# Cross-attention and quantised feed-forward on one core: tokens laid out with features on partitions, LayerNorm 1 folded into Wq and the query bias, token parts made a step ahead

## The reference, cut to what matters

```python
def _layernorm(x, eps=1e-05): ...           # (x - mean) / sqrt(var + eps) over the 512 features
def _ln(t, w, b): ...                       # the same over the 32 features of a head, with gain and shift

def xattn(x, y):
    y_main, y_dca = y[:, :-16], y[:, -16:]
    q = _ln((x @ Wq + bq) by head, qn_w, qn_b)
    k = _ln((y_main @ Wk + bk) by head, kn_w, kn_b);   v = y_main @ Wv + bv
    k_dca = _ln(keys of (y_dca @ Wkv_dca + bkv_dca), kn_dca_w, kn_dca_b);   v_dca = its values
    ctx = softmax(q k' * SCALE) v + softmax(q k_dca' * SCALE) v_dca      # two separate softmaxes
    return ctx @ Wo + bo

x = x + xattn(_layernorm(x), ctx_1024)
x = x + fake_quant(relu(fake_quant(_layernorm(x)) @ fake_quant(kernel) + fake_quant(bias)))   # 8 bits
```

## Time and profile before

| | |
|---|---|
| median of 3 runs | 368.29 us (367.71 to 371.18) |
| the profiled execution | 370.66 us, of which the span from the first to the last instruction is 368.8 us |
| busy share of the span | TensorE 87%, weight loads 70%, VectorE 85%, ScalarE 60%, GpSimd 47% |
| DMA | 39.14 MB moved, mean 106 GB/s; HBM read 17.15 MB |
| from the k_t transposes of batch 2 (78.08 us) to those of batch 14 (302.51 us) | 224.43 us for 12 steps, 18.70 us each |

### The profile page before, as it was taken

The page is one execution under the profiler, slowest core; times in us unless marked ns, Lnnn a source line. Parts: engine busy times, 40 slices in busy tenths (PEclk is TensorE's granted clock), DMA queues, the critical chain, the costliest instruction groups (busy, mean ns, idle before and its releaser), DMA issues.

```text
span 368.8 us, 7583 instructions
## 1 busy us (share of the span) xinstructions
PE 319.3 (87%) x2338; PEld 257.3 (70%) x2353; DVE 315.0 (85%) x804; ACT 222.5 (60%) x444; POOL 174.3 (47%) x261
## 2 busy tenths in 40 slices
PE   1498989799989999999898999999998999868732
PEld 0345657688877878787787888878787878566620
DVE  2987899799979899989898998989998999975664
ACT  3357886366666767676758585848584856552501
POOL 5201513327281828282828281828282837281620
PEclk9999899699999999999999999999999999998985
DMA  8870458507070909190909082828292616180002
GB/s 267 263 265 1 82 121 142 125 29 163 15 177 11 194 22 191 34 199 18 195 17 189 31 139 81 128 93 130 92 135 84 123 54 123 54 145 2 28 0 85
DMA packets 36451, 39.14 MB, mean 106 GB/s; under 512 B 8760, under 2 KB 27452, under 8 KB 36412
## 3 DMA queue, kind: packets, MB, share of 16 engines
q1 hardware_dynamic: 36044, 38.40, 48.2%
q10 hardware_dynamic: 368, 0.27, 0.3%
HBM read 17.15 MB, written 4.72 MB: 59 GB/s over the span
## 4 chain that ended last, share of the span: by engine, by line
PE 52%; DMA 9%; SPq 7%; issue 7%; DVE 3%; ACT 2%; POOL 0%; ACTq 0%; DVEq 0%
PE bank L1323 26%; SPq L372 7%; PE bank L1440 7%; DMA q_stack<-q_lo 7%; PE bank L1409 4%; PE bank L1596 4%; PE bank L1606 2%; PE bank L1420 2%; PE bank L1421 2%; PE bank L1463 2%; PE bank L1493 1%; DMA k_stack<-k_lo 1%; ACT k_hi L606 1%; PE bank L1498 1%; PE bank L1455 1%
## 5 line engine op out<-in xcount | busy, mean ns | idle before, releaser
L1440 PE MATMUL bank<-v_aug,prob_store 128*128 128x66 f32 x512 | 68.6, 278 | 3.4 <-ACT prob_store L744 3.4
L511 POOL TENSOR_TENSOR k_lo<-wkv_raw,k_hi 128x448 f16<-128x448 f32 x16 | 16.7, 1042 | 113.8 <-issue 105.9
L1440 PEld LDWEIGHTS bank<-v_aug,prob_store 128*128 128x128 f32 x512 | 64.4, 195 | 5.9 <-ACT prob_store L744 4.6
L1056 DVE TENSOR_REDUCE neg_max<-bank 128x4 f32<-128x448 f32 (+1 forms) x128 | 45.2, 416 | 9.9 <-PE bank L1409 9.9
L755 ACT ACTIVATE wkv_raw<-bank,affine 128x448 f32<-128x448 f32 (+1 forms) x32 | 22.4, 747 | 42.4 <-PE bank L1493 42.1
L744 ACT ACTIVATE prob_store<-bank,exp_scale 128x512 f32<-128x512 f32 x64 | 41.6, 677 | 4.9 <-PE bank L1421 4.8
L530 POOL TENSOR_TENSOR finals<-seg_out 128x128 f32<-128x128 f32 x64 | 34.4, 546 | 13.7 <-DVE seg_out L1069 13.4
L1420 PE MATMUL bank<-q_stack,k_stack 128*128 128x128 f16 x256 | 33.9, 220 | 1.9 <-ACT maxT L606 1.9
L1421 PE MATMUL bank<-maxT,sel 128*128 128x128 bf16 x256 | 33.7, 219 | 0.0
L1420 PEld LDWEIGHTS bank<-q_stack,k_stack 128*128 128x128 f16 x256 | 26.4, 104 | 6.1 <-issue 3.9
L1069 DVE TENSOR_TENSOR seg_out<-bank,rden 128x256 f32<-128x256 f32 x64 | 27.2, 424 | 3.8 <-POOL finals L530 1.7
(11 more groups left out here) (213 smaller groups left out, 876.9 us busy)
## 6 DMA issues: line engine op xcount, KB each, us to landing
x_in<-in_x SPq DMA_DIRECT2D x16, 256.0 KB, 4.9
q_stack<-q_hi SPq DMA_DIRECT2D x32, 128.0 KB, 3.7
q_stack<-q_lo SPq DMA_DIRECT2D x32, 128.0 KB, 4.6
k_stack<-k_hi SPq DMA_DIRECT2D x32, 128.0 KB, 3.3
k_stack<-k_lo SPq DMA_DIRECT2D x32, 128.0 KB, 4.3
out<-finals SPq DMA_DIRECT2D x16, 256.0 KB, 3.8
y_in<-in_ctx SPq DMA_DIRECT2D x16, 128.0 KB, 4.6
y_dcaT<-in_x SPq DMA_DIRECT2D x8, 256.0 KB, 4.3
```

Of the source, the lines that this page charges most:

```text
L1056: v.tensor_reduce(neg_max[:, HG * gr:HG * (gr + 1), seg], s4[:, :, lo:hi], AX.X, ALU.max, negate=True).then_inc(max_ready.sem, 1)
L1440: last = mm(bank[6 + gr % 2][:, VW * h:VW * (h + 1)], probs[:, gr % 2, h], v_aug[:, Bt.parity, HG * gr + h], start=True, stop=True)
```

## The change

Six things change together.

1. The host passes four more arrays (`laid_out`): tokens and main context rows with features on partitions (`tokens_T`, 128 x 736 a batch), the DCA rows the same way (`dca_T`), the six norm vectors in one row, and the bias and norm columns as 14 columns. The transposes of tokens and DCA rows on TensorE, and `setup_columns`, go.
2. `xT_hi`, `yT_hi` are copies by ScalarE of what was loaded (`high_context`, `high_stream`); they are double-buffered and made for batch L, a step ahead of their use. `xT_lo`, `yT_lo` move from VectorE to GpSimd (`low_context`, `low_stream`), for batch A.
3. x goes into the q product raw. LayerNorm 1's mean is taken out of Wq once: `setup_sums` (TensorE) makes the mean over the 512 input features of every column of the head-centred Wq, `level_queries` (VectorE) subtracts it. Its scale is applied when the query bias is added (`biased_queries`). `x_norm` is not made any more; the statistics are still taken from `x_in`, so x is now loaded twice for this stage.
4. The DCA part of Wkv_dca is loaded in two halves and its keys are centred partly on GpSimd (`centred_dca`).
5. SyncE issues the token loads of a step after the residual and DCA value loads, not before the store of the step.
6. `x_plus` and `f_intT` get other buffers.

```diff
 # SyncE, per step
-                if L is not None and L.has(2):
-                    prev = L.back(2)
-                    sp.wait_ge(*xn_ready.of(prev))
-                    sp.dma_start(x_in[:, L.parity], x[L.index()]).then_inc(x_loaded.sem(L), 16)
-                    sp.wait_ge(*yT_ready.of(prev))
-                    sp.dma_start(y_in[:, L.parity], ctx[L.index()]).then_inc(y_loaded.sem(L), 16)
+                def tokens():
+                    if L is not None and L.has(2):
+                        prev = L.back(2)
+                        sp.wait_ge(*ln1_steps.of(prev, 2))
+                        sp.dma_start(x_in[:, L.parity], x[L.index()]).then_inc(x_loaded.sem(L), 16)
+                        for read in (xhi_ready, xlo_ready, yhi_ready, ylo_ready):
+                            sp.wait_ge(*read.of(prev))
+                        sp.dma_start(xy_in[:, L.parity], xyT[L.index()]).then_inc(xy_loaded.sem(L), 16)
+
+                if N is None or not N.has(2):
+                    tokens()
...
                     if N.has(2):
                         residual()
                         dca_values()
+                        tokens()
...
 # GpSimd
+                def low_tokens(lo, hi, src, loaded, hi_ready, used, done):
+                    pool.wait_ge(*loaded)
+                    pool.wait_ge(*hi_ready.of(A))
+                    if A.has(1):
+                        pool.wait_ge(*used.of(A.back(1)))
+                    g.tensor_tensor(lo[:].rearrange("p c n -> p (c n)"), src,
+                                    hi[:, A.parity].bitcast(FP32).rearrange("p c n -> p (c n)"), ALU.subtract
+                                    ).then_inc(done.sem, 1)
...
                         pool.wait_ge(*kstack_in.of(N.back(1)))
                         dca_columns(k_hi, kdca_hi)
                         dca_columns(k_lo, kdca_lo)
-                        low(k_lo, k_n, k_hi, kn_ready, khi_ready, kstack_in, klo_ready, MAIN)
+                if A is not None and not A.first():
+                    low_context()
+                    low_stream()
+                if N is not None and not N.first():
+                    low(k_lo, k_n, k_hi, kn_ready, khi_ready, kstack_in, klo_ready, MAIN)
...
 # ScalarE
+                def high_context(b):
+                    act.wait_ge(*((first_context.sem, 16) if b.first() else xy_loaded.of(b)))
+                    if b.has(2):
+                        act.wait_ge(*v_ready.of(b.back(2)))
+                    copy(flat(yT_hi[:, b.parity]), context_in(b.parity)).then_inc(yhi_ready.sem, 1)
...
+                if L is not None and L.has(2):
+                    high_context(L)
+                    high_stream(L)
                 if N is not None:
                     if N.first():
                         setup_dca(0)
...
+                if L is not None and L.second():
+                    high_context(L)
+                    high_stream(L)
...
 # VectorE
+            def level_queries():
+                dve.wait_ge(wqsum_ready.sem, 1)
+                level = bank[0][:, :].unsqueeze(1).to_broadcast([P, XC // 2, D])
+                for half in range(2):
+                    part = slice(XC // 2 * half, XC // 2 * (half + 1))
+                    v.tensor_tensor(wq_raw[:, part], wq_raw[:, part], level, ALU.subtract).then_inc(wq_levelled.sem, 1)
...
-                    v.tensor_tensor(q_raw[:, A.parity], bank[2][:, :], bias_full[:, 0], ALU.add
-                                    ).then_inc(qraw_ready.sem, 1)
+                    if A.first():
+                        dve.wait_ge(bias_copied.sem, 2)
+                    dve.wait_ge(*ln1_rstd.of(A))
+                    v.scalar_tensor_tensor(q_raw[:, A.parity], bank[2][:, :], x_rstd[:, A.parity:A.parity + 1],
+                                           bias_full[:, 0], ALU.mult, ALU.add).then_inc(qraw_ready.sem, 1)
...
 # TensorE
+            def setup_sums():
+                pe.wait_ge(tiles_made.sem, 8)
+                for c in range(XC):
+                    pe.wait_ge(wq_centred.sem, 1 if c < XC // 2 else 2)
+                    last = mm(bank[0][:, :], per_token[:].to_broadcast([P, P]), wq_raw[:, c, :], start=c == 0, stop=c == XC - 1)
+                last.then_inc(wqsum_ready.sem, 1)
...
-                    for c in range(YC):
-                        last = tr(bank[1][:, P * c:P * (c + 1)], y_in[:, p, P * c:P * (c + 1)], ident[:])
-                    last.then_inc(yT_ready.sem, 1)
...
-                    for c in range(XC):
-                        last = tr(bank[0][:, P * c:P * (c + 1)], x_norm[:, p, P * c:P * (c + 1)], ident[:])
-                    last.then_inc(xT_ready.sem, 1)
```

More of the change, by code:

```diff
@@ L339, in _ @@
                      bias_parts[:, part])
+            sp.dma_start(x_in[:, 1], x[1]).then_inc(x_loaded.sems[1], 16)
+            sp.dma_start(xy_in[:, 1], xyT[1]).then_inc(xy_loaded.sems[1], 16)
             load(fk_in, fk_raw[:], chunked(ffn_kernel))
+            load(wdv_in, wd_raw[:, :, 1], chunked(Wkv_dca)[:, :, D:2 * D])
             load(wo_in, wo_raw[:], chunked(Wo))
@@ L618, in _ @@
             load(biases_in, bias_heads[2 * H:3 * H], bkv_dca[0:D].rearrange("(h d) -> h d", d=HD))
-            for j in range(2):
-                load(dca_in, y_dca[:, j], ctx[8 * j:8 * (j + 1), MAIN:, :])
             s.preload_act_table_set("natural_log_exp_and_others")
@@ L811, in step @@
                     setup_dca(1)
-                if L is not None and not L.second():
-                    token_statistics()
+                if L is not None and L.has(2):
+                    token_statistics(L)
                 if Bt is not None:
@@ L1165, in step @@
                     setup_ffn_bias()
-                if A is not None:
-                    low_part(yT_lo, yT_hi, bank[1][:, 0:CD], yhi_ready, v_ready, A, ylo_ready)
-                    if A.first():
-                        setup_queries()
-                if Bt is not None and Bt.first():
-                    low_part(xT_lo, xT_hi, bank[0][:, :], xhi_ready, q_ready, A, xlo_ready)
+                if A is not None and A.first():
+                    setup_queries()
                 if Bt is not None:
@@ L1629 @@
     arrays, args = {}, []
-    for name in _INS:
-        a = np.ascontiguousarray(inputs[name])
+    for name, a in [(name, inputs[name]) for name in _INS] + list(laid_out(inputs).items()):
+        a = np.ascontiguousarray(a)
         arrays[f"in_{name}"] = a
```

270 lines of the change are left out of this document (129 added, 141 removed).

## The result

The changed kernel takes 379.74 us (median of 4 executions, 378.3 to 381.5) against 368.63 us: a ratio of 1.0269, 95% interval 1.0215 to 1.0323. It is slower by 2.7%; the forecast was no change (367.6 us), and the time lies outside the range of 360.0 to 373.5. The profiled execution took 380.59 us, with a span of 378.7. Every ratio in this document leaves out the executions that took over 1.5% more than the fastest of the same kernel, so for e5, e10 and e12, where that matters, the median of all executions stands beside it.

The account below looks back on a forecast made before the run. Steps were taken as bound by a loop from k_t transposes over the stacks' DMAs and `scores(0)` to the next k_t. Setup +7.7 us, steps -8.4 us: 368.29 - 0.7 = 367.6 us, range 360.0 to 373.5.

Parts of the forecast that it names:

- I take 0.15 us a step, near the low end, because the products have that cover.: Steps: low parts on GpSimd delay VectorE's k and q head products, about 1 us of cover; 0.15 us lost a step.
- rival C: Steps: GpSimd and VectorE collide every time, losing 0.85 us a step and cancelling the gain; 376.0 us, chance 0.12.
- The loads behind the stacks: Steps: x_in moves from behind q_lo to behind the DCA values; about 0.3 us a step of shorter wait.
- can't turn into a longer wait at `scores(0)`: Steps: token transposes, 0.65 us of TensorE, stand behind that wait, so removing them shortens the loop without lengthening it.
- Setup up to batch 0's squares: Setup, start to batch 0's squares: cost +1.1 us, bounds -0.6 and +2.8.
- These nearly cancel: Setup: earlier weights, loads and bias against added matmuls and VectorE passes; batch 0's q product within half a microsecond of before.
- The ScalarE term: Setup: two copies of batch 1 (1.0 us) stand ahead of the square of q on ScalarE; cost +1.1 us.
- Batch 1's k product: Setup: waits for GpSimd's low parts behind both DCA key parts; starts at about 45.8, 6.4 us later.
- Rival B: Faster: setup hides one of its two stalls, costing 3.5 us, and steps give 0.85 each; 361.6 us, chance 0.32.
- ScalarE's wait for batch 3: Setup, step 0: some 4 us wait for xy_in at about 60 us; batch 2's k_t transposes come 7.7 us later.
- Rival D: Steps: token loads land too late for ScalarE every time, or freed time doesn't come; 373.6 us, chance 0.08.
- The tail: End of the kernel: no token work is left in it, so nothing changes.

Follow-up runs that it names:

- e5: Changed kernel with the edits of e2, e3 and e4 together: ratio 0.9705 to the kernel before, median of all executions 360.71 us against 370.0.
- e10: e5 with batch 0's `low_stream()` and `token_scale(A)` behind `centred_dca()` on GpSimd: ratio 0.9695 to the kernel before, median of all executions 366.63 us.
- e12: e5 again, unchanged, on another chip: ratio 0.9712 to the kernel before, median of all executions 360.09 us against 370.11.
- e4: Changed kernel; from batch 2 yT_lo back on VectorE, xT_lo on GpSimd only after VectorE's q_t product: 372.2 us, ratio 1.0048 to the kernel before.
- e9: e5 with a step's token loads issued at its start, behind q_lo of the step before: 362.41 us, ratio 0.9788 to the kernel before.
- e7: Changed kernel with a step's token loads issued at its start, behind q_lo of the step before: 381.18 us, ratio 1.0317 to the kernel before.
- e15: Changed kernel, unchanged, run for a second profile: 48.9 us from the last k_t transposes to the end.
- e2: Changed kernel with batch 1's low parts ahead of k_lo of batch 0 on GpSimd: 372.57 us, ratio 1.0088 to the kernel before.
- e3: Changed kernel; in step 0 ScalarE copies batch 3's high parts behind the copy of maxT: 376.71 us, ratio 1.0188 to the kernel before.
- e11: Changed kernel with both low parts subtracted twice on GpSimd from batch 2 on: 384.97 us, ratio 1.0417 to the kernel before.

## Why the prediction was wrong

**The loss is the setup's, and the steps don't pay for it.** The prediction was 7.7 us of setup against 8.4 us of steps. Measured in three profiles each: 11.5 against 2.9. The steps' gain missed by 5.5 us and the setup by 3.8.

**The term that failed: "I take 0.15 us a step, near the low end, because the products have that cover."** The cover is there: with the collision gone the step is 17.78 us (e4), a gain of 0.91 where 0.85 was booked. But I priced what the two 512-column products would lose. They lose nothing (1.08 us each, as before). What GpSimd's low parts hold are the 32-column operations ahead of them, and the forecast priced none of these: 1.4 us a step, 1.6 with the one that the FFN scaling holds, of which 0.67 are left after the cover. That is 8.0 us in 12 steps, 6.2 more than booked, and the larger part of the error. It was in my own rows: the earlier trace rows is exactly a small operation, stretched from 0.19 to 1.02 us by a GpSimd operation of 1.04. I had it down as a sign for rival C and still gave C 0.12. The Trainium skill (page "SBUF — State Buffer", section "SBUF: two separate sides") states that a VectorE operation with two SBUF inputs and a GpSimd operation that reads SBUF exclude one another for the whole instruction. Applied to the small operations, that rule was the better forecast. The traces agree with it: L1079 and L1081 end 0.05 us behind the GpSimd operation that they meet, and the maxima, which read PSUM, take 1.41 us for four beside xT_lo in e4.

**Rival C** named the mechanism and nearly its size (0.85 us lost a step, 0.67 measured), and its 376.0 us is the nearest of the four. It was short by the setup (3.8 us); the steps gained a little where it gave them nothing.

**The loads behind the stacks** were booked at about 0.3 us of the 0.85. They are worth 0.18 where the loop is the bound (e9), and next to nothing in the changed kernel (e7). That the transposes' removal "can't turn into a longer wait at `scores(0)`" held: the idle there went from 0.87 us to nothing. It turned into a wait further on, at the q_t transposes.

**Setup up to batch 0's squares:** +1.1 booked, +2.8 measured at k_t of batch 0. "These nearly cancel" was wrong: the q product of batch 0 started at 28.00, 29.45 and 28.95 us in the three profiles of the changed kernel, against 26.54, 25.28 and 28.67, 2.0 us later by the means. The ScalarE term was nearly right: from the q product to its square it is 0.9 us more by the means, 1.1 booked. What holds the q product differs between the profiles. In the first one the new mean over the input features (`setup_sums`, L1404) takes 3.67 us, and the levelling (L1002) starts only at 24.38, behind VectorE's list of small operations, of which GpSimd had stretched L974 to 1.72 us from 0.16 before; the centring of Wq ahead of it had taken 3.35 us (2.89 before, 2.36 in e10). e10 shows that one of these two can be taken away, and that the other place then pays. In the other two profiles the same sums take 6.41 and 6.58 us, and the levelling waits for them. TensorE's and VectorE's timelines of e15:

```profile
18.85 6.41 PE L1404 MATMUL bank<-wq_raw,per_token 128*128 128x512 f32 x8 [1.42 <-DVE wq_raw L936]
...
25.29 2.35 DVE L1002 TENSOR_TENSOR wq_raw<-wq_raw,bank 128x1024 f32<-128x1024 f32 x2 [0.60 <-PE bank L1404]
```

That is what the prediction had as its upper bound of 2.8, the sums at twice their time. Why they take it in some executions no row shows: the granted clock reads 1.00 from 16 to 30 us in all three. The first four DCA products of the kernel before vary in the same way, 3.50, 1.98 and 3.78 us.

**Batch 1's k product:** right. Predicted at 45.8 with GpSimd's yT_lo as the releaser; it started at 47.40 (the 1.6 are the first stretch's error), and e2 shows that nothing else was behind those 6.3 us. Rival B, which needed this wait or the next to be hidden, falls.

**ScalarE's wait for batch 3:** right in place and size (about 4 us at about 60; 4.40 us up to 66.93). But it was priced as if all of it reached the steps; e3 took it out and got 2.2 us at batch 2's k_t transposes. In that profile a longer stretch at half clock follows; that it took the place of the wait is likely, not shown.

**Rival D,** ScalarE waiting for xy_in in every step: the wait is there (12.3 us in all) and costs nothing (e7).

**The tail** was right at no change; the first profile of the changed kernel alone would have charged it with 2.8 us.

**What was open** is the share of the clock in the setup. Apart from the stall ahead of batch 1's k product (e2), the three stretches before batch 2 have half-clock windows in some executions and not in others, of both kernels, and I can't give them a part of the 11.5 us.

## What to carry to other kernels

Moving work to an idle engine was not free here, where both engines use SBUF. List the operations that the moved one will run beside: the first small, chained one that it met lost nearly the moved operation's own length (0.41 us to one of 0.66, 1.03 us to one of 1.29), and the wide ones behind them nothing. In an order that is in line per engine, a producer "a step ahead" is late in the first steps, where nothing is ahead yet: follow each queue through batches 0 to 3 by hand. The costs in the steps, at batch 1's k product and at batch 3's tokens went away by placement alone (e5 and e12, 2.5 to 2.7% faster than the kernel before), so a change that measures slower may hold a gain.

## What the runs showed of the hardware

- With GpSimd's operation under way VectorE's next one with two SBUF inputs ends just behind it (0.05 us for the small ones). The other way round, two VectorE operations without a gap hold GpSimd for both: its 1.29 us became 2.90 to 2.94 in all 12 steps of e11. In a chain of small operations with gaps GpSimd got in between some and not between others.
- The size of the held operation doesn't matter: L974 (3 columns) took 1.72 us beside GpSimd's 1.91 us, and in e10 L986 (one column) 1.19. And L1171, which has a single tensor input from SBUF, took 0.45 instead of 0.17 us and ended with GpSimd's L574 (176.83 and 176.79).
- The row of the granted clock doesn't show every change of TensorE's speed: it reads 1.00 from 16 to 30 us in three profiles of one kernel in which the same eight matmul records take 3.67, 6.41 and 6.58 us.
- TensorE's granted clock fell to half after an idle of about 2 us in some executions of one kernel and not in others, at the same place of the program. The same code then took 3.8 us longer in the setup (e5, e12) and 2.6 us longer in the tail (48.7 to 51.3). So a difference of 3 us between single profiles of a kernel of this length says nothing by itself.
